# Gathers of the second batch tile without waits, and early layer-0 work placed in other units of a DLRM tower kernel

## The chip, the cores and the metric

One core of a Trainium2 chip. The metric is the device time of one execution of the program, in microseconds (us); of several executions the median is taken. The profile is of one execution.

## The reference

For 2048 samples, 32 embedding rows of 16 numbers are looked up. Three layers of a compressed interaction network follow, then a small dense tower. Cut to what matters:

```python
e = jnp.stack([tbl_f[ids[:, f]] for f in range(32)], axis=1)   # 2048 x 32 x 16
x0 = xk = e
for W in (W0, W1, W2):                                          # each 32 x (32 or 64) x 64
    xk = jax.nn.relu(jnp.einsum('bmd,bhd,mhk->bkd', x0, xk, W))
    outs.append(jnp.sum(xk, axis=2))
h = jnp.concatenate(outs + [dense_ctx], axis=1)
h = jnp.maximum(h @ W_top1 + b_top1, 0.0)
h = jnp.maximum(h @ W_top2 + b_top2, 0.0)
y = h @ W_top3
```

Everything is float32; matmuls of the layers are float32 matmuls.

## The kernel before, in words

The batch is cut into 16 tiles of 128 samples. A tile has 16 embedding columns; 128 samples times 4 columns make a block of 512 columns (64 blocks), and two blocks make a pair (32 pairs, two to a tile). The main loop runs over 256 units (L565 on ACT, L679 on DVE, L876 on PE, L384 on POOL), four units to a block, and each unit has four places i = 0 to 3. Written as (unit, i), the tables at L41 to L44 say where work on a pair is put; an entry (o, i) of pair p means unit 8(p-1)+o.

Names used below. A(n) is the DVE product of layer 1 for unit n, and B(q) that of layer 2, made in unit q+6 (L663, 128x2048 each; DVE does A(n), then B(n-6)). x1(s) and x2(s) are the outputs of layer 0 and layer 1 for block s, taken out of PSUM by ACT (L475, L490); A(4s) to A(4s+3) need x1(s), B(4s) to B(4s+3) need x2(s). Each has one buffer, so x1(s) also waits for A(4s-1) to be done and x2(s) for B(4s-1). PE multiplies each product with the weights in four contractions (L773), layer 1 on one half of the array's columns and layer 2 on the other; a contraction of layer 1 and one of layer 2 run side by side. A product of layer 1 may lie three units ahead of PE, one of layer 2 two (L661).

Layer 0 of a pair is made of squares. PE turns the pair's columns (`turn`, L699), ACT copies them (`take_x0`), PE forms sums of fields in five tiles t0 to t4 (`sum_fields`, L723), ACT squares each (`square`, L458), and PE contracts each square with a layer-0 weight (`l0_tile`, L732). Two square buffers lie between ACT and PE. When t4 is contracted, x1 of the pair's blocks can be taken. The first square of a pair also copies the fields, which an ACT DMA stores to memory; SP then loads these rows spread over the partitions into a ring of ten buffers (`keep_rows`, L264), 1 MB to a unit, and DVE reads them as one operand of A and B.

The embeddings come by 32 indirect gathers to a tile, issued by POOL (L306), into two buffers by turns. ACT casts the gathered tile to bf16 (`split_high`, L444), POOL subtracts (`split_rest`), ACT casts the rest (`split_mid`, L450), and POOL subtracts again (`split_low`); then the tile's pairs can be turned. Tile 0 is split by ACT and DVE ahead of the loop. Tile 1 is gathered in four portions that each wait for another thing (L377); then POOL runs split_rest and split_low of tile 1, and only then its loop, in which the gathers of tile 2 and later are issued a few per unit after A(n-1) is done (L390 to L395), with the additions of layer sums between them (L397 to L404).

All of this is one order written out by hand for each engine; engines work theirs in order and wait on semaphores.

```python
TURN_AT = {1: (1, 3), 2: (3, 0), 4: (0, 0)}
SPLIT_AT = {1: (9, 10), 2: (4, 5)}
```

SPLIT_AT gives the units, counted within the 16 units of a tile, in which ACT runs split_high and split_mid at i = 1: for tile 1 units 9 and 10, for tile 2 units 20 and 21. The places of x2 are made by `x2_at` (L91): x2(0) at (5, 0), x2(1) at (9, 0), x2(2) at (13, 0), x2(4) at (20, 3).

Of the kernel before, what the change touches and what calls it, by code (L numbers as in the profile page):

```python
# [14 lines left out]
B, M, D, K = 2048, 32, 16, 64  # L15
NB = 128
BT = B // NB
# [9 lines left out]
OFF = 6  # L27
# [10 lines left out]

TURN_AT = {1: (1, 3), 2: (3, 0), 4: (0, 0)}  # L41
SUMS_AT = {1: [(2, 1), (4, 0), (4, 3), (5, 1), (5, 3)], 2: [(3, 2), (4, 0), (4, 2), (5, 0), (5, 2)]}
L0_AT = {1: [(4, 1), (4, 3), (5, 1), (5, 3), (6, 1)], 2: [(4, 1), (4, 3), (5, 1), (5, 3), (6, 1)]}
X1_AT = {1: (6, 2), 2: (6, 2)}  # L44
for later in range(3, PAIRS):
    TURN_AT.setdefault(later, (-1, 1))
    SUMS_AT[later] = [(0, 2) if later == 4 else (0, 0), (1, 1), (2, 2), (4, 0), (4, 3)]
    L0_AT[later] = [(3, 0), (3, 2), (4, 2), (5, 0), (5, 2)]
    X1_AT[later] = (6, 0)


def places(table):

    at = {}
    for p, where in table.items():
        for t, (o, i) in enumerate(where if isinstance(where, list) else [where]):
            at[8 * (p - 1) + o, i] = (p, t)
    return at


TURNS, SUMS, L0S, X1S = (places(table) for table in (TURN_AT, SUMS_AT, L0_AT, X1_AT))

SPLIT_AT = {1: (9, 10), 2: (4, 5)}
for later in range(3, BT):
    SPLIT_AT[later] = (1, 4)
PIECES = 9
GROUPS = [(2 * g, 2) for g in range(7)] + [(14, 1), (15, 1)]
LAST_GROUP = len(GROUPS) - 1
# [3 lines left out]
def pieces_at():  # L72

    at = {}
    for g, (first, tiles) in enumerate(GROUPS[:-1]):
        ready = 16 * (first + tiles - 1) + 31
        for q in range(PIECES):
            if g < LAST_GROUP - 2:
# [12 lines left out]
def x2_at():  # L91

    at = {}
    for s in range(BLOCKS):
        at[(4 * s + OFF - 2, 3) if s % 2 == 0 and s >= 4 else (4 * s + OFF - 1, 0)] = s
    return at


X2S = x2_at()


# [5 lines left out]
def tower(nc, dense_t, ids, tables, w_top1, b_top1, w_top2, b_top2, w_top3, w0_pairs, w0_all, w1, w2,  # L107
          sel_sums, identity, x0_rows, out):
    with ExitStack() as ctx:
# [6 lines left out]
        def sem(name):  # L116
            return ctx.enter_context(nc.semaphore(name))
# [39 lines left out]
        at = 2 * (ST + 1) * K  # L157
# [38 lines left out]
        s_turn0 = sem("first_turned")  # L196
# [18 lines left out]
        s_prod = {1: sem("prod1_ready"), 2: sem("prod2_ready")}  # L215
        s_done = {1: sem("unit1_done"), 2: sem("unit2_done")}
        s_x = {1: sem("x1_ready"), 2: sem("x2_ready")}
# [80 lines left out]
        def _(pool):  # L298
            def gather(t, lo, hi):
                if lo == 0 and t == 2:  # L300
                    pool.wait_ge(s_high0, len(first_splits))
                    pool.wait_ge(s_rest0, len(first_splits))
                elif lo == 0 and t > 2:
                    pool.wait_ge(s_high, t - 2)
                    pool.wait_ge(s_rest, t - 2)
                for m in range(lo, hi):  # L306
                    pool.indirect_dma_start(  # L307
                        emb[t % 2][:, m, :], None, tables[m],
                        bass.IndirectOffsetOnAxis(ap=idx[:, t, m:m + 1].bitcast(U32), axis=0)
                    ).then_inc(s_early if t == 0 and m < EARLY else s_gather[t % 2], 16)  # L310

            def split_rest(t):
                pool.wait_ge(s_high, t)
                pool.tensor_tensor(rest[:, :, :], emb[t % 2][:, :, :].rearrange("p m d -> p d m"),  # L314
                                   parts[:, :, 0, :], ALU.subtract).then_inc(s_rest, 1)

            def split_low(t):
                pool.wait_ge(s_mid, t)
                pool.tensor_tensor(parts[:, :, 2, :], rest[:, :, :], parts[:, :, 1, :],
                                   ALU.subtract).then_inc(s_low, 1)  # L320
# [53 lines left out]
            gather(0, 0, M)  # L374
            pool.wait_ge(s_ids, 16)

            for k, (ready, count) in enumerate(((s_turn0, 2), (s_x[1], 1), (s_prod[1], 4), (s_prod[1], 6))):  # L377
                pool.wait_ge(ready, count)
                gather(1, k * M // 4, (k + 1) * M // 4)

            split_rest(1)
            split_low(1)
# [1 line left out]
            for n in range(10, LAST):  # L384
                t = n // 16 + 1
                if 2 <= t < BT and n % 16 == SPLIT_AT[t][0] + 1:
                    split_rest(t)
                if 2 <= t < BT and n % 16 == SPLIT_AT[t][1] + 1:
                    split_low(t)
# [19 lines left out]
        def _(act):  # L409
# [34 lines left out]
            def split_high(t):  # L444
                tile0 = M - EARLY if t % 2 == 0 else M
                act.wait_ge(s_gather[t % 2], 16 * (tile0 + M * (t // 2)))
                nc.scalar.copy(parts[:, :, 0, :], emb[t % 2][:, :, :].rearrange("p m d -> p d m"))\  # L447
                    .then_inc(s_high, 1)

            def split_mid(t):  # L450
                act.wait_ge(s_rest, t)
                nc.scalar.copy(parts[:, :, 1, :], rest[:, :, :]).then_inc(s_mid, 1)

            def take_x0(p):
                act.wait_ge(s_wide, 6 * (p - 1) + 1)
                nc.scalar.copy(x0[p % 2][:, :, :], wide[:, :, :]).then_inc(s_took, 1)  # L456
# [33 lines left out]
            def take_x2(s):  # L490
                act.wait_ge(s_done[1], 4 * s + 4)
                if s:
                    act.wait_ge(s_prod[2], 4 * s)
                if halved(1, s):
                    src = [(accs[64 * c:64 * c + 64, s % 2, 0:HALF], slice(HALF * c, HALF * c + HALF))
                           for c in range(2)]
                else:
                    src = [(accs[0:64, s % 2, :], slice(0, BLK))]
                for half in range(2):
                    for bank, cols in src:  # L500
                        last = nc.scalar.activation(xp[2][64 * half:64 * half + 64, cols], bank, ACT.Relu)  # L501
                last.then_inc(s_x[2], 1)
                if s >= 6:
                    act.wait_ge(s_z12, (s - 6) // 4 + 1)
                for bank, cols in src:
                    last = nc.scalar.activation(zin[64:128, s % 6, cols], bank, ACT.Relu)  # L506
                last.then_inc(s_xz[2], 1)

            def take_x3(s):
                act.wait_ge(s_done[2], 4 * s + 4)  # L510
                if s >= 4:
                    act.wait_ge(s_z3, s // 4)
                if halved(2, s):
                    for c in range(2):
                        last = nc.scalar.activation(x3[:, s % 4, HALF * c:HALF * c + HALF],
                                                    accs[64 * c:64 * c + 64, s % 2, 0:HALF], ACT.Relu)
                else:
                    last = nc.scalar.activation(x3[:, s % 4, :], accs[64:128, s % 2, :], ACT.Relu)  # L518
                last.then_inc(s_xz[3], 1)
# [45 lines left out]
            for n in range(LAST):  # L565
                for i in range(GT):
                    t = n // 16 + 1
                    if i == 1 and t < BT and n % 16 == SPLIT_AT[t][0]:
                        split_high(t)
                    if i == 1 and t < BT and n % 16 == SPLIT_AT[t][1]:  # L570
                        split_mid(t)
                    if (n, i) in X2S:
                        take_x2(X2S[n, i])
                    if n % 4 == (OFF + 4) % 4 and i == 0 and n >= OFF + 4:
                        take_x3((n - OFF - 4) // 4)
                    if (n, i) in TURNS:
                        take_x0(TURNS[n, i][0])
                    if (n, i) in SUMS:
                        square(*SUMS[n, i])
                    if n % 8 == 2 and i == 0 and n + 2 < UNITS:  # L580
                        take_x1((n + 2) // 4)
                    if (n, i) in X1S:
                        take_x1(2 * X1S[n, i][0])
                    if (n, i) in PIECES_AT:
                        g, q = PIECES_AT[n, i]
                        if q < 4 or q == 8:
                            take_event(g, min(q, 6))
                        elif q % 2:
                            take_event(g, 4 + (q - 4) // 2)
# [367 lines left out]
```

## Time and profile before

| | us |
|---|---|
| median of three executions | 1262.93 |
| lowest and highest of them | 1252.1 and 1274.45 |
| the profiled execution | 1259.4 |
| its span in the profile | 1257.6 |
| PE busy, DVE busy, ACT busy, POOL busy | 1204.9, 1147.8, 522.5, 682.7 |

The span is what the profile shows of the execution; the remaining 1.8 us lie around it. PE is the matmul engine, DVE the vector engine, ACT the scalar engine, POOL the gather engine here, SP the engine that issues the row loads. A float32 matmul of the program shows as two records in the trace. A matmul's record includes a modelled end, so records overlap; the step from one start to the next is the price of one.

### The profile page before, as it was taken

The numbers are of one execution on the slowest core, as the hardware profiler recorded it, in microseconds if no ns is written. First come the engines' busy times: TensorE is split into PE (matmuls) and PEld (weight loads), VectorE is DVE, ScalarE is ACT, GpSimd is POOL, SyncE is SP. The second block draws the span as 40 slices with busy tenths as digits, with TensorE's granted clock in tenths as the row PEclk, the third lists the DMA queues.
The fourth block names the chain that finished last, engine by engine and source line by source line (L and its number), as shares of the span: only waits on it lengthen the run. The fifth ranks groups of instructions, "written<-read, shape, count | busy, mean of one in ns | idle before, by whom it ended". The sixth has DMA issues, their size and how long they took to land.

```text
span 1257.6 us, 16644 instructions
## 1 busy us (share of the span) xinstructions
PE 1204.9 (96%) x6396; PEld 615.6 (49%) x6396; DVE 1147.8 (91%) x534; ACT 522.5 (42%) x786; POOL 682.7 (54%) x705
## 2 busy tenths in 40 slices
PE   0899989999999999999999999999999999999998
PEld 0442424445555555555555555555555555555444
DVE  3388989999999999999999999999999999999894
ACT  0445344434453443444344444444443444444321
POOL 6665776866767474755647375564737551210101
PEclk9999989999999999999999999999999999999998
DMA  5388978888889888898899999999998999999850
GB/s 120 78 232 224 219 197 247 248 247 236 250 237 242 235 242 239 237 240 243 226 226 229 233 246 246 248 245 236 247 243 233 228 234 241 238 235 235 210 135 1
DMA packets 73685, 277.50 MB, mean 221 GB/s; under 512 B 29819, under 2 KB 38805, under 8 KB 41318
## 3 DMA queue, kind: packets, MB, share of 16 engines
q1 hardware_dynamic: 54388, 267.09, 82.2%
q0 software_dynamic: 16384, 4.23, 3.3%
q10 hardware_dynamic: 2834, 5.12, 1.6%
q8 instruction: 51, 0.84, 0.3%
q14 instruction: 28, 0.23, 0.1%
HBM read 272.15 MB, written 4.20 MB: 220 GB/s over the span
## 4 chain that ended last, share of the span: by engine, by line
PE 88%; POOL 5%; issue 3%; DVE 2%; ACT 1%; DMA 1%; ACTq 0%; POOLq 0%; DVEq 0%
PE accs L789 66%; PE acc L743 10%; POOL emb L307 4%; PE wide L712 4%; PE xe L800 2%; DVE prod L663 2%; PE xe L809 2%; PE wide L695 1%; PE acc L856 1%; DMA emb<-in_tbl,idx 1%; PE wide L719 0%; PE wide L809 0%; PE xe L819 0%; ACT xe L501 0%; DMA idx<-in_ids 0%
## 5 line engine op out<-in xcount | busy, mean ns | idle before, releaser
L789 PE MATMUL accs<-prod,w2s 128*64 128x512 f32 x2016 | 936.3, 595 | 3.1 <-DVE prod L663 2.8
L789 PE MATMUL accs<-prod,w1s 128*64 128x512 f32 x2016 | 930.5, 594 | 0.7 <-DVE prod L663 0.7
L663 DVE TENSOR_TENSOR prod<-kept,xe 128x2048 f32<-128x2048 f32 x256 | 583.7, 2281 | 48.9 <-PE accs L789 30.9
L307 POOL DMA_INDIRECT emb<-in_tbl,idx x512 | 484.5, 946 | 204.4 <-issue 118.6
L663 DVE TENSOR_TENSOR prod<-kept,xp 128x2048 f32<-128x2048 f32 x256 | 583.1, 2279 | 6.8 <-ACT xp L482 6.8
L789 PEld LDWEIGHTS accs<-prod,w1s 128*64 128x64 f32 x2016 | 271.9, 137 | 313.6 <-issue 194.2
L789 PEld LDWEIGHTS accs<-prod,w2s 128*64 128x64 f32 x2016 | 269.8, 137 | 72.5 <-issue 40.7
L468 ACT ACTIVATE sq<-wide 128x1024 f32<-128x1024 f32 (+1 forms) x155 | 145.5, 939 | 171.9 <-PE wide L712 82.4
L743 PE MATMUL acc<-sq,u 128*64 128x512 f32 x640 | 200.5, 596 | 5.2 <-ACT sq L468 4.9
L346 POOL TENSOR_TENSOR x3f<-x3f 64x512 f32<-64x512 f32 x31 | 39.6, 1277 | 137.1 <-ACT x3f L518 136.9
L743 PEld LDWEIGHTS acc<-sq,u 128*64 128x64 f32 x640 | 82.8, 137 | 60.9 <-issue 15.7
L518 ACT ACTIVATE x3f<-accs 64x512 f32<-64x512 f32 x63 | 37.4, 593 | 126.9 <-PE accs L789 126.8
L712 PE MATMUL wide<-x,sums 128*64 128x512 bf16 x500 | 86.2, 380 | 0.6 <-ACT sq L468 0.5
L314 POOL TENSOR_TENSOR rest<-emb,parts 128x512 f32<-128x512 f32 x15 | 21.3, 1423 | 118.7 <-ACT parts L447 118.7
L501 ACT ACTIVATE xe<-accs 64x512 f32<-64x512 f32 (+1 forms) x130 | 73.1, 562 | 24.0 <-DVE prod L663 22.2
L456 ACT CAST x<-wide 128x1024 bf16<-128x1024 f32 x31 | 31.4, 1012 | 103.9 <-PE wide L695 103.9
L326 POOL TENSOR_TENSOR zin<-zin 128x512 f32<-128x512 f32 x32 | 41.2, 1286 | 59.1 <-ACT zin L506 58.8
L712 PEld LDWEIGHTS wide<-x,sums 128*64 128x64 bf16 x500 | 36.3, 110 | 67.5 <-issue 58.5
L466 ACT COPY x3f<-wide 32x1024 f32<-32x1024 f32 x31 | 31.0, 999 | 69.5 <-PE wide L712 69.4
L481 ACT ACTIVATE xp<-acc 64x512 f32<-64x512 f32 x64 | 36.4, 568 | 43.8 <-DVE prod L663 36.1
L856 PE MATMUL acc<-u 128*128 128x384 f32 x32 | 13.3, 578 | 35.5 <-DMA emb<-in_tbl,idx 35.5
L506 ACT ACTIVATE zin<-accs 64x512 f32<-64x512 f32 (+1 forms) x65 | 37.9, 583 | 1.6
(85 smaller groups left out, 510.7 us busy)
## 6 DMA issues: line engine op xcount, KB each, us to landing
kept<-x_rows SPq DMA_DIRECT2D x252, 512.0 KB, 5.3
kept<-x_rows SPq DMA_DIRECT2D x504, 256.0 KB, 6.5
emb<-in_tbl,idx POOLq DMA_INDIRECT x512, 2.6
x_rows<-x3f ACTq DMA_DIRECT2D x31, 128.0 KB, 4.7
prod<-in_w_all ACTq DMA_DIRECT2D x1, 512.0 KB, 6.7
w1s<-in_L_rec_W SPq DMA_DIRECT2D x4, 128.0 KB, 3.3
w2s<-in_L_rec_W SPq DMA_DIRECT2D x4, 128.0 KB, 3.5
wt<-in_W_top SPq DMA_DIRECT2D x1, 512.0 KB
```

The source lines that it names most:

```text
L307: pool.indirect_dma_start(emb[t % 2][:, m, :], None, tables[m], bass.IndirectOffsetOnAxis(ap=idx[:, t, m:m + 1].bitcast(U32), axis=0)).the ...
L326: pool.tensor_tensor(zin[:, a, :], zin[:, a, :], zin[:, a + 1, :], ALU.add).then_inc(s_zp, 1)
L346: pool.tensor_tensor(x3[:, a, :], x3[:, a, :], x3[:, a + 1, :], ALU.add).then_inc(s_z3p, 1)
L468: nc.scalar.activation(sq[k % 2][:, 0:n, :], wide[:, 0:n, :], ACT.Square).then_inc(s_took, 1)
L481: nc.scalar.activation(xp[1][0:64, :], src, ACT.Relu)
L501: last = nc.scalar.activation(xp[2][64 * half:64 * half + 64, cols], bank, ACT.Relu)
L506: last = nc.scalar.activation(zin[64:128, s % 6, cols], bank, ACT.Relu)
L518: last = nc.scalar.activation(x3[:, s % 4, :], accs[64:128, s % 2, :], ACT.Relu)
L663: nc.vector.tensor_tensor(prod[layer][:, q % BUFS[layer], :, :], kept[:, q % KEPT, :, :], xp[layer][:, :].unsqueeze(1).to_broadcast([128, ...
L712: last = mm(bank[64 * c:64 * c + 64, :], sums[:, t, 64 * c:64 * c + 64], x0[p % 2][:, j, :], start=True, stop=True)
L743: last = mm(acc0[64 * j:64 * j + 64, :], w, squares, start=t == 0, stop=t == ST - 1)
L789: last = mm(accs[64 * (layer - 1):64 * layer, s % 2, :], wk[layer][:, t, :], prod[layer][:, q % BUFS[layer], i, :], start=t == 0, stop=t = ...
```

## The change

- POOL issues the 32 gathers of tile 1 right behind those of tile 0, with none of the four waits.
- ACT takes x2(0) at (4, 0) where it was (5, 0).
- ACT casts tile 1 in unit 8: split_high at (8, 1), split_mid at (8, 2), where they were at (9, 1) and (10, 1).
- Pair 1 (the second): sums and squares t0 to t4 at (2,1), (3,3), (4,1), (4,3), (5,1), and layer-0 contractions at (4,0), (4,2), (5,0), (5,2), (5,3).
- Pair 2 (the third): turn at (10, 0) where it was (11, 0); sums and squares from (10, 2) to (13, 2) where they were from (11, 2) to (13, 2); layer-0 contractions from (11, 3) to (14, 0) where they were from (12, 1) to (14, 1).
- The places of later pairs, and the number of instructions of each kind, stay.

```diff
-L0_AT = {1: [(4, 1), (4, 3), (5, 1), (5, 3), (6, 1)], 2: [(4, 1), (4, 3), (5, 1), (5, 3), (6, 1)]}
+L0_AT = {1: [(4, 0), (4, 2), (5, 0), (5, 2), (5, 3)], 2: [(3, 3), (4, 1), (4, 3), (5, 2), (6, 0)]}
...
-SPLIT_AT = {1: (9, 10), 2: (4, 5)}
+SPLIT_AT = {1: (8, 8), 2: (4, 5)}
...
+MID_TILE = {1: 2}
...
-        at[(4 * s + OFF - 2, 3) if s % 2 == 0 and s >= 4 else (4 * s + OFF - 1, 0)] = s
+        at[(4, 0) if s == 0 else (4 * s + OFF - 2, 3) if s % 2 == 0 else (4 * s + OFF - 1, 0)] = s
...
-            for k, (ready, count) in enumerate(((s_turn0, 2), (s_x[1], 1), (s_prod[1], 4), (s_prod[1], 6))):
-                pool.wait_ge(ready, count)
-                gather(1, k * M // 4, (k + 1) * M // 4)
+            gather(1, 0, M)
...
-                    if i == 1 and t < BT and n % 16 == SPLIT_AT[t][1]:
+                    if t < BT and n % 16 == SPLIT_AT[t][1] and i == MID_TILE.get(t, 1):
                         split_mid(t)
```

With the new `x2_at`, x2(2) stands at (12, 3), where it was at (13, 0); at both places it comes behind the square t2 of pair 2 and ahead of t3.

Line numbers of the changed kernel are one smaller than before on ACT and PE. ACT, from the first square of pair 1 (sq) through x2(0) (xe<-accs, in four pieces), before:

```order
L468 ACTIVATE sq<-wide 128x1024
L472 DMA x_rows<-x3f 32x2x512
L468 ACTIVATE sq<-wide 128x1024 x2
L501 ACTIVATE xe<-accs 64x256 x4
L506 ACTIVATE zin<-accs 64x256 x2
L468 ACTIVATE sq<-wide 128x1024
L468 ACTIVATE sq<-wide 128x512
L481 ACTIVATE xp<-acc 64x512
```

and now:

```order
L467 ACTIVATE sq<-wide 128x1024
L471 DMA x_rows<-x3f 32x2x512
L467 ACTIVATE sq<-wide 128x1024
L500 ACTIVATE xe<-accs 64x256 x4
L505 ACTIVATE zin<-accs 64x256 x2
L467 ACTIVATE sq<-wide 128x1024 x2
L467 ACTIVATE sq<-wide 128x512
L480 ACTIVATE xp<-acc 64x512
```

x2(0) and its copy for the sums (zin) have moved ahead of the square t2, behind t1 alone.

ACT from x1(2) in unit 6 on, where parts<-emb is split_high and parts<-rest is split_mid of tile 1, before:

```order
L481 ACTIVATE xp<-acc 64x512
L482 ACTIVATE xp<-acc 64x512
L488 ACTIVATE zin<-acc 64x512
L501 ACTIVATE xe<-accs 64x512 x2
L506 ACTIVATE zin<-accs 64x512
L447 CAST parts<-emb 128x16x32
L518 ACTIVATE x3f<-accs 64x512
L481 ACTIVATE xp<-acc 64x512
L482 ACTIVATE xp<-acc 64x512
L488 ACTIVATE zin<-acc 64x512
L452 CAST parts<-rest 128x16x32
L456 CAST x_0<-wide 128x1024
```

and now:

```order
L480 ACTIVATE xp<-acc 64x512
L481 ACTIVATE xp<-acc 64x512
L487 ACTIVATE zin<-acc 64x512
L446 CAST parts<-emb 128x16x32
L451 CAST parts<-rest 128x16x32
L500 ACTIVATE xe<-accs 64x512 x2
L505 ACTIVATE zin<-accs 64x512
L517 ACTIVATE x3f<-accs 64x512
L455 CAST x_0<-wide 128x1024
L480 ACTIVATE xp<-acc 64x512
L481 ACTIVATE xp<-acc 64x512
L487 ACTIVATE zin<-acc 64x512
```

Both casts of tile 1 now stand together ahead of x2(1), and the copy of turned pair 2 (x_0<-wide) stands ahead of x1(3) (the second xp pair).

PE around the layer-0 contractions t2, t3 and t4 of pair 1 (acc<-sq,u, two matmuls each; w1s and w2s are contractions of layers 1 and 2), before:

```order
L743 MATMUL acc<-sq,u 64x512 x2
L789 MATMUL accs<-prod,w1s 64x512 x2
L719 MATMUL wide<-x_1,sums 64x512 x2
L743 MATMUL acc<-sq,u 64x512 x2
L789 MATMUL accs<-prod,w1s 64x512
L789 MATMUL accs<-prod,w2s 64x512
L789 MATMUL accs<-prod,w1s 64x512
L789 MATMUL accs<-prod,w2s 64x512
L743 MATMUL acc<-sq,u 64x512 x2
```

and now:

```order
L788 MATMUL accs<-prod,w1s 64x512
L742 MATMUL acc<-sq,u 64x512 x2
L788 MATMUL accs<-prod,w1s 64x512
L718 MATMUL wide<-x_1,sums 64x512 x2
L788 MATMUL accs<-prod,w1s 64x512
L742 MATMUL acc<-sq,u 64x512 x2
L788 MATMUL accs<-prod,w1s 64x512
L742 MATMUL acc<-sq,u 64x512 x2
L788 MATMUL accs<-prod,w1s 64x512
```

The contraction t4 has moved ahead of unit 6, whose first two pairs of contractions stood ahead of it.

## Rows read from the trace of the kernel before

**Rows 1.** Busy time by stretch, with the granted clock and DMA.

```profile
core 0: us, PE busy (x) PEld busy (x) DVE busy (x) ACT busy (x) POOL busy (x), PEclk, DMA share, GB/s
160.00:170.00 10.00, 7.84 (x26) 2.46 (x28) 8.57 (x4) 4.79 (x9) 8.16 (x9) 0.66 0.51 135
200.00:300.00 100.00, 100.00 (x502) 45.99 (x500) 99.52 (x47) 43.81 (x63) 68.28 (x71) 1.00 0.87 243
600.00:700.00 100.00, 100.00 (x528) 52.52 (x526) 97.31 (x46) 43.77 (x64) 61.18 (x63) 1.00 1.00 230
```

**Rows 2.** What DVE waited for, 58 to 182 us: total, times, longest.

```profile
DVE prod L663 <- ACT xe L501: 12.7, 4, 6.5
DVE prod L663 <- ACT xp L482: 6.8, 4, 2.3
DVE prod L663 <- PE accs L789: 0.5, 1, 0.5
```

**Rows 3.** What DVE waited for, 182 us to the end.

```profile
DVE prod L663 <- PE accs L789: 30.4, 33, 2.0
```

**Rows 4.** Timeline of DVE: start, length, and in brackets the idle time before.

```profile
78.87 2.29 DVE L663 TENSOR_TENSOR prod<-kept,xe 128x2048 f32<-128x2048 f32 x1 [3.68 <-ACT xe L501]
...
86.69 2.29 DVE L663 TENSOR_TENSOR prod<-kept,xp 128x2048 f32<-128x2048 f32 x1 [1.14 <-ACT xp L482]
...
116.77 2.29 DVE L663 TENSOR_TENSOR prod<-kept,xe 128x2048 f32<-128x2048 f32 x1 [1.43 <-ACT xe L501]
...
125.76 2.29 DVE L663 TENSOR_TENSOR prod<-kept,xp 128x2048 f32<-128x2048 f32 x1 [2.30 <-ACT xp L482]
...
160.91 2.29 DVE L663 TENSOR_TENSOR prod<-kept,xe 128x2048 f32<-128x2048 f32 x1 [6.49 <-ACT xe L501]
...
180.30 2.29 DVE L663 TENSOR_TENSOR prod<-kept,xe 128x2048 f32<-128x2048 f32 x1 [1.11 <-ACT xe L501]
```

**Rows 5.** Timeline of PE.

```profile
70.85 0.64 PE L789 MATMUL accs<-prod,w1s 128*64 128x512 f32 x1 [0.74 <-DVE prod L663]
...
105.71 0.62 PE L695 MATMUL wide<-ident_b,parts 128*128 128x128 bf16 x8 [0.23 <-POOL parts L319]
106.26 0.64 PE L789 MATMUL accs<-prod,w1s 128*64 128x512 f32 x1
...
108.02 0.60 PE L712 MATMUL wide<-x,sums 128*64 128x512 bf16 x4
108.45 0.59 PE L789 MATMUL accs<-prod,w1s 128*64 128x512 f32 x1
...
112.12 1.03 PE L743 MATMUL acc<-sq,u 128*64 128x512 f32 x4
```

**Rows 6.** Timeline of ACT.

```profile
70.03 1.02 ACT L468 ACTIVATE sq<-wide 128x1024 f32<-128x1024 f32 x1
...
77.37 1.46 ACT L501 ACTIVATE xe<-accs 64x256 f32<-64x256 f32 x4
...
85.50 0.57 ACT L481 ACTIVATE xp<-acc 64x512 f32<-64x512 f32 x1 [2.78 <-PE acc L743]
...
158.66 1.04 ACT L447 CAST parts<-emb 128x512 bf16<-128x512 f32 x1 [7.40 <-DMA emb<-in_tbl,idx]
```

**Rows 7.** Timeline of POOL.

```profile
48.47 0.94 POOL L307 DMA_INDIRECT emb<-in_tbl,idx  x1 [4.43 <-PE wide L695]
...
98.60 1.41 POOL L314 TENSOR_TENSOR rest<-emb,parts 128x512 f32<-128x512 f32 x1 [10.41 <-ACT parts L447]
104.50 1.16 POOL L319 TENSOR_TENSOR parts<-rest,parts 128x512 bf16<-128x512 f32 x1 [4.49 <-ACT parts L452]
...
144.09 1.29 POOL L326 TENSOR_TENSOR zin<-zin 128x512 f32<-128x512 f32 x1
...
148.23 0.96 POOL L307 DMA_INDIRECT emb<-in_tbl,idx  x1
...
150.74 0.94 POOL L307 DMA_INDIRECT emb<-in_tbl,idx  x1 [0.30 <-issue]
```

**Rows 8.** What SP's DMA queue waited for, whole span.

```profile
SPq L270 <- DVE prod L663: 624.8, 215, 9.4
```

More of the change, by code:

```diff
@@ L37 @@
 WARM = 16
-TURN_AT = {1: (1, 3), 2: (3, 0), 4: (0, 0)}
-SUMS_AT = {1: [(2, 1), (4, 0), (4, 3), (5, 1), (5, 3)], 2: [(3, 2), (4, 0), (4, 2), (5, 0), (5, 2)]}
-L0_AT = {1: [(4, 1), (4, 3), (5, 1), (5, 3), (6, 1)], 2: [(4, 1), (4, 3), (5, 1), (5, 3), (6, 1)]}
+TURN_AT = {1: (1, 3), 2: (2, 0), 4: (0, 0)}
+SUMS_AT = {1: [(2, 1), (3, 3), (4, 1), (4, 3), (5, 1)], 2: [(2, 2), (3, 1), (4, 0), (4, 3), (5, 2)]}
+L0_AT = {1: [(4, 0), (4, 2), (5, 0), (5, 2), (5, 3)], 2: [(3, 3), (4, 1), (4, 3), (5, 2), (6, 0)]}
 X1_AT = {1: (6, 2), 2: (6, 2)}
```

## The prediction

> **What bounds the kernel now.** Busy time by stretch comes first [rows 1]. From 200 to 300 us DVE is busy for 99.5 of 100 us, from 600 to 700 us for 97.3 of 100, with PE at 100 in both. So the early units go at the pace of DVE, the later ones at that of PE. What DVE waited for says the same: after 182 us nearly all of its waiting is for PE, 30.4 us in 33 short pieces [rows 3]; before that it waited 20.0 us, 12.7 for ACT's x2, 6.8 for x1 and 0.5 for PE [rows 2]. The change touches only units 4 to 20, which lie before 182 us. A microsecond of DVE waiting that goes there shifts all that follows, and as PE later has the same work to do from an earlier start, the end moves with it. So the sum is one over DVE's idle pieces.
>
> Each of them has its row [rows 4]: 3.68 us at 78.87 (B(0), waiting for x2(0)), 1.14 at 86.69 (A(8), x1(2)), 1.43 at 116.77 (B(8), x2(2)), 2.30 at 125.76 (A(16), x1(4)), 6.49 at 160.91 (B(16), x2(4)), 1.11 at 180.30 (B(20), x2(5)). With the 0.5 us on PE that is 16.7; most of the rest is the wait for x1(1) in unit 4, which nothing here moves. Between waits DVE runs at 2.20 us a product: from 86.69 to the wait before 116.77 thirteen products take 28.65 us, the last one's end counted in.
>
> Why B(16) is late stands with ACT and POOL. ACT was free at 158.66 - 7.40 = 151.26 and waited for tile 2's gathers before it could cast and then take x2(4) [rows 6]. The last of these gathers was issued at 150.74 [rows 7], so it landed 7.9 us later. POOL issued it so late because it had stood idle for 10.41 us, then 4.49 us, for ACT's two casts of tile 1, with tile 2's gathers queued behind [rows 7]. PE ran dry as well, and its granted clock fell: from 160 to 170 us it is busy for 7.84 us and the mean clock is 0.66, so for most of that stretch it was at 1.2 GHz, not 2.4 [rows 1].
>
> **Prices on PE** [rows 5]. A sum is 0.43 us (108.02 to 108.45), half of it for t4. From 106.26 to 108.02 stand two pairs of contractions, so a pair is about 0.86, and a layer-0 tile is four records of the same shape, 0.86 too. The turn is 0.55. A contraction of layer 1 alone also costs 0.86: half the array stands idle.
>
> **Term 1, units 4 to 8.** The square t0 of pair 1 still ends at 71.05 [rows 6]. PE does sum t1 at 71.1, now ahead of unit 4; its square ends at about 72.8, and x2(0), 1.46 us for four pieces [rows 6], at 74.3. DVE is free for B(0) at 78.87 - 3.68 = 75.2, so this wait goes. What is late next is x1(2). PE must do the eight lone contractions of units 4 and 5, five layer-0 tiles and the sums t1 to t4: 13 x 0.86 + 3 x 0.43 + 0.22 = 12.7 us, so t4 is contracted at 83.8. As a test, before it ran from 70.85 [rows 5] with 12.7 plus the two pairs of unit 6, 14.4, and x1(2) began at 85.50 [rows 6], 0.2 later. So now x1(2) begins at 84.0 and A(8) at 85.2. DVE, with B(0), A(7), B(1) done, is free at 81.8 and waits 3.4 us. Of the 4.8 us of two waits 3.4 come back as one: the gain is 1.5 us, not 4.8. Bounds: 0, if PE loses its 1.7 us at small waits, and 4.8.
>
> **Term 2, units 8 to 16.** The gathers of tile 1 begin at about 44.3 instead of 48.47 and issue every 1.25 us [rows 7], so the last goes out at 83.1 and, at the 7.9 us of tile 2's last, has landed by 91.0, likelier by 87. ACT waits for it behind x1(2) with nothing due until x2(1) at 94. Casts and subtractions (1.05, 1.4, 0.6, 1.2) are done by some 90.5, at the latest 95.5, against 105.7. The turn of pair 2 in unit 10 thus waits for nothing but B(4), which ends at 85.2 + 5 x 2.20 + 2.29 = 98.5. Then pair and turn to 99.9, ACT's copy to 101.1, x1(3) to 102.3 (A(12) wants it at 102.8), field copy and square t0 to 104.8. PE does sum t1 to 105.3, the rest of unit 11 and tile t0 to 107.9, then in unit 12 four pairs, two sums and two tiles, 6.0 us, to 113.9. The square t2 ends near 110.3. x2(2) therefore waits only for B(7), whose end is 111.7, and is out at 112.9; B(8) wants it at 85.2 + 28.65 = 113.9. The 1.43 us go. Unit 13 on PE (four pairs, sum t4, tile t3: 4.5 us) ends at 118.4, pair and tile t4 at 120.1, x1(4) at 121.5. DVE is free for A(16) after three products, at 120.5, and waits 1.0 of its former 2.30. A(16) comes at 121.5 against 125.76: 4.3 us are gained so far, 2.8 of them here. Bounds for this term: 0 (one slip of PE behind a square) and 3.7.
>
> **Term 3, unit 20.** POOL is free for tile 2 from 90.5, but a gather waits for A(n-1), three or four a unit, so it goes with DVE now. Units 10 to 18 hold 29 gathers; in unit 18 also the additions, 4.1 us (144.09 to 148.23 [rows 7]). POOL begins the four gathers of unit 17 at about 124.3, those of unit 18 at 129.3, and after the additions the last three at 137.2; the last goes out at 139.7, 11 us earlier. Landing takes 7.9 us if it is as slow as before: 147.6. ACT arrives at 151.26 - 4.3 = 147.0. DVE, free at 121.5 + 28.65 = 150.2, needs x2(4) then, so the cast must start by 150.2 - 1.15 - 1.05 = 148.0. It does, with 0.4 us to spare at the slowest landing that the rows show. All 6.49 us go. Bounds: 3 us, if the landing takes over 11 us, and 6.49.
>
> On this landing the Trainium skill (DMA: Bandwidth & Descriptors, section Anatomy of one DMA — SWDGE (gpsimd) path) gives 2.0 us plus bytes over 436 GB/s; for a gather of 8 KB that is an estimate of 2.0 us, by which the last would land at 141.7, the sum would stay as it is and the rival of a late landing would fall away. The trace has 7.9 us at this place, so the rival keeps its chance.
>
> **Term 4, after the stall.** The 0.5 us on PE and part of the 1.11 us at B(20) come from PE's half clock and the backlog of it. I take 1.1 of 1.6; bounds 0 and 1.6.
>
> **Sum.** 1.5 + 2.8 + 6.5 + 1.1 = 11.9 us. The profiled execution took 1259.4 (span 1257.6), so 1247.5; I say 1248. The profiled one is 3.5 us below the median of 1262.93, of which 1248 is 1.2% less.
>
> **Rivals.**
> - The placing does nothing: PE in units 4 to 14 slips at each square and terms 1 and 2 are 0. For it speaks that they rest on margins of about a microsecond; against it that no wait of theirs takes PE's place in the chain worked out above. 1259.4 - 6.5 - 1.1 = 1251.8.
> - The gathers of tile 2 still land late: past 148.0 each microsecond of landing costs one. Kept are terms 1 and 2 alone: 1259.4 - 4.3 = 1255.1. For it the 0.4 us margin, against it the 11 us of earlier issue.
> - The row loads become the bound, from unit 10 to the end. A unit needs 1.05 MB in 4.40 us, 238 GB/s; 243 were moved from 200 to 300 us and 230 from 600 to 700. There DVE's 97.31 us busy are 44.2 products, 22.1 units, so PE's pace is 4.52 us a unit [rows 1]. Should 228 be all that comes, a unit takes 4.60 us: 0.20 more than DVE's over units 10 to 47, 7 us, and 0.08 more than PE's over the 208 units behind, 17 us: 1248 + 24 = 1272, slower than before. It decides at about 230 GB/s (4.55 us a unit), where the 11.9 us are used up. Against it: the loads waited 624.8 us for DVE to free a buffer [rows 8], so the 230 is what was asked for, and none of DVE's waits before 182 us is for a load [rows 2].
> - More goes than I count: all of the 16.7 us, 1259.4 - 16.7 = 1242.7; against it the 12.7 us of PE work in term 1.
>
> **Chances.** Forecast 0.61, placing without effect 0.14, late landing 0.14, row loads 0.04, all waits gone 0.07. From 1242.7 to 1255.1 hold nearly all of it; but three executions of the same kernel lie 22 us apart, 0.9% to either side of their median, so the range goes some 8 us beyond either end: 1236 to 1263. Two per cent of the median, about what a measurement of this kernel can tell from no change, is 25 us: no case reaches 1237.7, only scatter on top of a full gain does. Faster by over 2%: 0.11; within: 0.86; slower: 0.03.
>
> **What would show it.** DVE should have one wait of about 3.4 us before A(8) at 85, one of about 1 before A(16), none at B(0), B(8) and B(16); ACT no wait for gathers in unit 20; POOL's gathers of tile 1 in one row from 44 to 84 us; PE's clock full from 150 to 180 us. Wrong would be: x2(4) still behind the gathers, A(8) still at 86.7, a DVE wait on row loads, or a gain that is there at 182 us and gone at 300.

## The result and the profile after

| | before | after |
|---|---|---|
| median of 20 executions each, us | 1259.84 | 1252.38 |
| lowest and highest, us | 1252.1 and 1274.45 | 1247.48 and 1265.31 |
| the profiled execution, us | 1259.4 | 1254.39 |
| its span, us | 1257.6 | 1252.6 |

The ratio of the times, which leaves out executions over 1.5% above the fastest of their kernel, is 0.9944, with a 95% interval from 0.9924 to 0.9965: faster by 0.6%, some 7 us, which lies within 2%. The forecast was 1248 in a range from 1236 to 1263.

What DVE waited for from 58 to 182 us, after (total, times, longest):

```profile
DVE prod L662 <- ACT xp L481: 7.2, 4, 3.3
DVE prod L662 <- ACT xe L500: 1.8, 2, 1.1
DVE prod L662 <- PE accs L788: 0.6, 1, 0.6
```

Those are 9.6 us, against 20.0 before [rows 2]. x2 costs 1.8 us where it cost 12.7; x1 has gone up from 6.8 to 7.2 (3.3 us of either are A(0)'s 2.04 and A(4)'s 1.28, which the change leaves alone). The timeline of DVE shows the places:

```profile
84.69 2.29 DVE L662 TENSOR_TENSOR prod<-kept,xp 128x2048 f32<-128x2048 f32 x1 [3.30 <-ACT xp L481]
...
118.45 2.29 DVE L662 TENSOR_TENSOR prod<-kept,xe 128x2048 f32<-128x2048 f32 x1 [0.55 <-PE accs L788]
121.32 2.29 DVE L662 TENSOR_TENSOR prod<-kept,xp 128x2048 f32<-128x2048 f32 x1 [0.58 <-ACT xp L481]
...
151.09 2.29 DVE L662 TENSOR_TENSOR prod<-kept,xe 128x2048 f32<-128x2048 f32 x1 [1.11 <-ACT xe L500]
...
169.48 2.29 DVE L662 TENSOR_TENSOR prod<-kept,xe 128x2048 f32<-128x2048 f32 x1 [0.72 <-ACT xe L500]
```

They are A(8), B(9), A(16), B(16) and B(20). The waits of 3.68 us at B(0) and 1.43 at B(8) [rows 4] are gone; B(16) keeps 1.11 of 6.49. ACT after:

```profile
72.38 1.46 ACT L500 ACTIVATE xe<-accs 64x256 f32<-64x256 f32 x4
...
83.51 0.57 ACT L480 ACTIVATE xp<-acc 64x512 f32<-64x512 f32 x1 [2.78 <-PE acc L742]
...
91.39 1.09 ACT L446 CAST parts<-emb 128x512 bf16<-128x512 f32 x1 [6.22 <-DMA emb<-in_tbl,idx]
...
148.79 1.09 ACT L446 CAST parts<-emb 128x512 bf16<-128x512 f32 x1 [1.97 <-DMA emb<-in_tbl,idx]
```

x2(0) is taken at 72.38 instead of 77.37, x1(2) at 83.51 instead of 85.50, and the last cast starts at 148.79 instead of 158.66 [rows 6]. POOL after:

```profile
82.97 0.94 POOL L308 DMA_INDIRECT emb<-in_tbl,idx  x1 [0.30 <-issue]
92.56 1.41 POOL L315 TENSOR_TENSOR rest<-emb,parts 128x512 f32<-128x512 f32 x1 [8.64 <-ACT parts L446]
94.70 1.16 POOL L320 TENSOR_TENSOR parts<-rest,parts 128x512 bf16<-128x512 f32 x1 [0.73 <-ACT parts L451]
96.02 0.95 POOL L308 DMA_INDIRECT emb<-in_tbl,idx  x1 [0.15 <-DVE prod L662]
...
140.92 0.94 POOL L308 DMA_INDIRECT emb<-in_tbl,idx  x1 [0.31 <-issue]
```

The last gather of tile 1 (82.97), the two subtractions of tile 1, the first gather of tile 2 (96.02) and its last (140.92; 150.74 before [rows 7]). Busy time by stretch, in the columns of [rows 1]:

```profile
160.00:170.00 10.00, 9.78 (x53) 3.75 (x51) 9.28 (x5) 4.70 (x6) 8.46 (x9) 1.00 1.03 245
200.00:300.00 100.00, 99.04 (x494) 45.77 (x492) 96.87 (x45) 44.42 (x64) 67.12 (x69) 1.00 1.03 233
600.00:700.00 100.00, 100.00 (x530) 52.62 (x528) 98.12 (x46) 43.51 (x64) 60.41 (x63) 1.00 0.96 243
```

From 160 to 170 us PE is at 2.4 GHz throughout (1.00; 0.66 before) and busy for 9.78 us instead of 7.84. But from 200 to 300 us DVE is busy for 96.87 us instead of 99.52, and the DMA share is 1.03 at 233 GB/s, where it was 0.87 at 243 [rows 1]. What is missing there stands in DVE's waits after 182 us:

```profile
DVE prod L662 <- PE accs L788: 27.1, 29, 2.0
DVE prod L662 <- DMA kept<-x_rows: 7.2, 21, 0.7
```

The second row is new: 7.2 us in 21 pieces for the row loads. Before has no such row.

**Where the 5.0 us between the two profiled spans come from.** Take A(30), the seventh product behind B(20), whose wait is the last that the change touches, and B(255), the last product of all. On DVE's timeline, before:

```profile
195.69 2.28 DVE L663 TENSOR_TENSOR prod<-kept,xp 128x2048 f32<-128x2048 f32 x1
...
1238.96 4.48 DVE L663 TENSOR_TENSOR prod<-kept,xe 128x2048 f32<-128x2048 f32 x2
```

and after:

```profile
184.88 2.28 DVE L662 TENSOR_TENSOR prod<-kept,xp 128x2048 f32<-128x2048 f32 x1
...
1238.74 2.28 DVE L662 TENSOR_TENSOR prod<-kept,xe 128x2048 f32<-128x2048 f32 x1
```

The row of 1238.96 holds B(254) and B(255); B(255) starts 2.20 later, at 1241.16. A(30) starts at 195.69 before and 184.88 after, 10.8 us earlier, 0.5 of which A(0) already had (58.31 and 57.80; over all the profiles of this document it lies between 57.8 and 59.0). From A(30) to B(255) before takes 1045.47 us and after 1053.86: 8.4 us lost. The end behind B(255) is 2.6 us shorter after. 0.5 + 10.3 - 8.4 + 2.6 = 5.0. The last term is the clock: one group of matmuls near the end, on PE's timeline, before:

```profile
1250.62 3.68 PE L809 MATMUL wide<-h,wt 128*64 128x128 f32 x32 [0.69 <-ACT h L539]
```

and after:

```profile
1247.73 1.97 PE L808 MATMUL wide<-h,wt 128*64 128x128 f32 x32 [0.69 <-ACT h L538]
```

The same 32 matmuls took 3.68 us at 1.2 GHz (granted clock 0.50 from 1250 to 1254 us) and 1.97 at 2.4 (1.00). Behind B(255) a profile takes either 13.8 us or 16.4 to 16.8, and both kernels have both: the changed one has the long end in e4 and e9 below, the kernel before the short one in e6. So the 2.6 us are not put down to the change. The 8.4 us are the question of the experiments.

### The profile page after: what moved, and what is told of

Its sections match the earlier page's. It is cut to its first block, busy times and chain, and to the rows that moved or that the text cites. A ratio compares the mean times of both kernels' runs of the same rounds, so it can differ in the third digit from the quotient of the medians.

```text
span 1252.6 us, 16643 instructions
## 1 busy us (share of the span) xinstructions
PE 1204.9 (96%) x6396; PEld 606.0 (48%) x6396; DVE 1150.4 (92%) x534; ACT 522.6 (42%) x786; POOL 682.9 (55%) x705
## 4 chain that ended last, share of the span: by engine, by line
PE 72%; DMA 12%; DVE 6%; POOL 5%; issue 4%; SPq 1%; ACT 0%; DVEq 0%; ACTq 0%
PE accs L788 54%; DMA kept<-x_rows 11%; PE acc L742 9%; DVE prod L662 6%; POOL emb L308 5%; PE wide L711 3%; PE xe L799 2%; PE xe L808 2%; PE wide L694 1%; SPq L271 1%; DMA emb<-in_tbl,idx 1%; PE wide L718 0%; PE xe L818 0%; DMA idx<-in_ids 0%; PE accs L784 0%
## 5 line engine op out<-in xcount | busy, mean ns | idle before, releaser
L742 PE MATMUL acc<-sq,u 128*64 128x512 f32 x640 | 218.9, 593 | 0.3 <-ACT sq L437 0.3
L711 PE MATMUL wide<-x,sums 128*64 128x512 bf16 x500 | 90.0, 380 | 1.1 <-ACT sq L467 1.0
```

Of the source, the lines that this page charges most:

```text
L711: last = mm(bank[64 * c:64 * c + 64, :], sums[:, t, 64 * c:64 * c + 64], x0[p % 2][:, j, :], start=True, stop=True)
L742: last = mm(acc0[64 * j:64 * j + 64, :], w, squares, start=t == 0, stop=t == ST - 1)
```

## The experiments

Theory A: the loads take back what the change gains, since products that come earlier ask for rows earlier than they can come; the kernel before loses nothing to them. The theory that stood in the end, D in the later expectations: the loads have slow stretches that come and go in either kernel, so an execution loses between 0 and 16 us whether or not the change is in it. Every time below is a median of several executions unless it is said to be one execution; losses, waits and distances from A(0) are each read from one profile. All products and the row loads are found again by their order, so "loss" below always means the time from A(30) to B(255) less 1045.4 us, which is what it takes when no product waits for a load.

**e1 and e2: a quarter of the row loads left out.** In both kernels the last of the three row loads of a unit (32 of 128 partitions) is left out from unit 14 on; the products there use what an earlier unit left in the ring.

```diff
-                for r, lo, hi in PARTS:
+                for r, lo, hi in PARTS if n < KEPT + MADE else PARTS[:2]:
...
-                        dve.wait_ge(s_kept[q % KEPT], 48 * loads)
+                        dve.wait_ge(s_kept[q % KEPT], 48 + 32 * (loads - 1))
```

Before with it:

> The kernel before, with the last of the three row loads of a unit (256 KB of 1 MB, partitions 96 to 127) left out from unit 14 on, so these partitions hold old rows. Theory A (in the changed kernel the row loads take back most of what was gained, and only because DVE no longer pauses; in the kernel before they cost nothing): DVE had no wait on a load before, so the time stays within 0.4% of before, 1254 to 1262 us; the wait at B(16), where tile 2's gathers land late, may shrink from 6.5 us to some 3. Theory B (the loads bound both kernels all along): over 8 us faster than before, under 1251.

Measured: 1253.27 us, ratio 0.9937 [0.9909, 0.9966], loss 0. Both theories' numbers were missed by a little: the kernel before had no load wait to lose in its first profile, and still gained. 6.0 us of the gain are at A(30), and they come from the gathers. Timeline of ACT, e1:

```profile
153.94 1.08 ACT L447 CAST parts<-emb 128x512 bf16<-128x512 f32 x1 [2.32 <-DMA emb<-in_tbl,idx]
```

The last gather of tile 2 was issued at 151.07 and the cast ran at 153.94: landed 2.9 us after its issue, not 7.9. The wait before B(16) shrank from 6.49 to 1.45 us. So 5.0 us of the stall that the change removes were themselves the work of the row loads, which hold the gathers up.

After with it:

> The changed kernel with the same load left out from unit 14 on. Theory A: no DVE wait on a load, the gain of 10.8 us that the changed kernel shows at A(30) is kept to the end: 1245 to 1249 us, 0.990 to 0.993 of before. Rival C (it is PE or ACT that gives the gain back between 250 and 585 us): DVE waits on PE there instead, and the time stays near 1252.

Measured: 1245.67 us, ratio 0.9879 [0.9827, 0.9932], loss 0, as either theory has it once the loads are light; A(30) is 126.05 us behind A(0), against 137.38 in before and 131.35 in e1. Busy time by stretch, e2:

```profile
200.00:300.00 100.00, 100.00 (x504) 48.33 (x502) 98.74 (x46) 45.60 (x67) 68.98 (x71) 1.00 0.62 189
```

With the DMA share at 0.62 nothing waits for a load, and the whole early gain arrives at B(255) (by the clock of the span, 10.85 us ahead of before at A(30) and 10.91 there). Against e1 the change is worth 7.6 us between medians; in the profiles it is 5.3 at A(30), the rest being the clock of the tail, which costs e1 2.6 us (3.68 us for the 32 matmuls, 1.97 in e2). Between the executions with a mean granted clock of 0.999 or more (five of e1, three of e2) the medians are 1250.5 and 1245.5, 5.0 apart.

**e3: the gathers and casts alone.** The changed kernel with the old tables for pairs 1 and 2 and the old places of x2(0) and x2(2).

```diff
-SUMS_AT = {1: [(2, 1), (3, 3), (4, 1), (4, 3), (5, 1)], 2: [(2, 2), (3, 1), (4, 0), (4, 3), (5, 2)]}
+SUMS_AT = {1: [(2, 1), (4, 0), (4, 3), (5, 1), (5, 3)], 2: [(3, 2), (4, 0), (4, 2), (5, 0), (5, 2)]}
...
-        at[(4, 0) if s == 0 else (4 * s + OFF - 2, 3) if s % 2 == 0 else (4 * s + OFF - 1, 0)] = s
+        at[(4 * s + OFF - 2, 3) if s % 2 == 0 and s >= 4 else (4 * s + OFF - 1, 0)] = s
```

> The kernel before with the new gathers of tile 1 and the casts in unit 8, but all pairs and x2(0) at their old places. If the four terms are right: waits at B(0) 3.7, A(8) 1.1, B(8) about 1 and A(16) about 2 us stay, the one at B(16) falls from 6.5 to under 1, A(30) starts 6.5 to 8 us earlier than before, near 188 us. Theory A: then loads take part of it back and the end comes at 1253 to 1257. If the places were needed for it: the wait at B(16) stays above 3 us.

Measured: 1257.21 us, ratio 0.9961 [0.9927, 0.9994]. The waits at B(0), A(8), B(8) and A(16) stand (3.68, 1.14, 1.14, 2.30 us), that at B(16) is gone, and A(30) comes 129.77 us after A(0), 7.6 earlier than before: just terms 3 and 4 of the sum. Its profile then lost 14.4 us.

**e4: the changed kernel again.** No edit.

> The changed kernel, unchanged, in another execution. Theory A: DVE again waits for row loads somewhere between 200 and 600 us, 4 to 10 us in all, and the gain of some 11 us at A(30) is down to 3 to 6 at the end. Rival D (a slow stretch of the memory that the first profile met by chance): no such waits, or at another place, and the gain at the end is 9 us or more.

Measured: 1255.66 us, ratio 0.9953 [0.9912, 0.9993]. Its profile gained as much by A(30) (127.03 us from A(0)) and lost 15.8. What DVE waited for from 182 us on, e4:

```profile
DVE prod L662 <- DMA kept<-x_rows: 12.8, 25, 1.2
```

That is more than either expectation had: 13 of the pieces lie between 203 and 317 us, the other 12 between 954 and 1035. Busy time by stretch, e4:

```profile
700.00:750.00 50.00, 50.00 (x280) 27.85 (x277) 47.66 (x23) 21.25 (x33) 29.78 (x31) 1.00 0.84 236
950.00:1000.00 50.00, 47.36 (x243) 24.46 (x240) 43.65 (x20) 19.45 (x29) 28.54 (x30) 1.00 1.03 214
```

From 700 to 750 us the loads have room: 236 GB/s at a share of 0.84, and DVE waits for none from 600 to 900. From 950 to 1000 they bring 214 GB/s at a share of 1.03, and DVE is busy for 43.65 us instead of 47.66. The loop asks for 1 MB of rows a unit at both places.

**e5 and e6: the kernel before, two more executions.** No edit.

> The kernel before, unchanged, in another execution. Theory A (DVE's pauses before 182 us keep the ring of row buffers full, so loads never cost the kernel before anything): no DVE wait on a load, as in its first profile. Theory D (stretches in which the memory serves the loads more slowly come at any time and cost either kernel): in at least one of two such looks DVE waits for loads over 3 us in all, after 182 us. The wait at B(16) for tile 2's gathers should be 4 to 8 us in both theories.

> The same again, a third execution of the kernel before: theory A no DVE wait on a load, theory D over 3 us in this one or the other. The wait at B(16) 4 to 8 us.

Measured: one execution each, 1265.21 and 1269.75 us, losses 4.9 and 12.0; B(16) waits 5.81 and 6.80 us, as expected. What DVE waited for from 182 us on, e5:

```profile
DVE prod L663 <- PE accs L789: 29.3, 32, 2.0
DVE prod L663 <- DMA kept<-x_rows: 4.6, 9, 0.8
```

and e6:

```profile
DVE prod L663 <- PE accs L789: 27.8, 31, 2.0
DVE prod L663 <- DMA kept<-x_rows: 10.2, 15, 1.8
```

Busy time by stretch, e6:

```profile
700.00:750.00 50.00, 50.00 (x277) 28.65 (x275) 47.66 (x23) 21.31 (x33) 26.53 (x27) 1.00 0.85 235
950.00:1000.00 50.00, 46.44 (x235) 21.37 (x233) 43.49 (x21) 18.77 (x28) 30.75 (x33) 1.00 1.03 213
```

213 GB/s at a share of 1.03, as in e4 at the same place, where the first profile of before moves 236 GB/s at 0.98 and has no such wait. Theory A falls in its second half: the kernel before loses to the loads too. Its first profile, on which the prediction was built, was an execution that lost nothing.

**e7: pair 1 alone.** The kernel before with the new places of pair 1 and x2(0) at (4, 0).

```diff
-L0_AT = {1: [(4, 1), (4, 3), (5, 1), (5, 3), (6, 1)], 2: [(4, 1), (4, 3), (5, 1), (5, 3), (6, 1)]}
+L0_AT = {1: [(4, 0), (4, 2), (5, 0), (5, 2), (5, 3)], 2: [(4, 1), (4, 3), (5, 1), (5, 3), (6, 1)]}
```

(with the new SUMS_AT of pair 1 and the x2(0) place likewise)

> The kernel before with only pair 1's new places and x2(0) at (4, 0). By term 1 the wait at B(0) goes, the one at A(8) grows to 3.3 us, and A(8) starts 26.9 us after A(0) instead of 28.4, 1.5 us earlier. The waits at B(8) 1.4, A(16) 2.3 and B(16) 4 to 8 us stay. The rival, that PE loses it to small waits: A(8) 28.4 us after A(0).

Measured: one execution, 1270.16 us. Timeline of DVE, e7:

```profile
85.42 2.29 DVE L663 TENSOR_TENSOR prod<-kept,xp 128x2048 f32<-128x2048 f32 x1 [3.30 <-ACT xp L482]
...
115.60 2.29 DVE L663 TENSOR_TENSOR prod<-kept,xe 128x2048 f32<-128x2048 f32 x1 [1.43 <-ACT xe L501]
...
124.59 2.29 DVE L663 TENSOR_TENSOR prod<-kept,xp 128x2048 f32<-128x2048 f32 x1 [2.30 <-ACT xp L482]
...
159.86 2.29 DVE L663 TENSOR_TENSOR prod<-kept,xe 128x2048 f32<-128x2048 f32 x1 [6.61 <-ACT xe L501]
```

A(8) waits 3.30 us and comes 26.89 us after A(0), as in the changed kernel and 1.5 earlier than before; B(8), A(16) and B(16) wait as before. A(30) is 2.0 us nearer to A(0). Then 15.2 us went to loads: a part of the change that gains 2 us came out 11 us over the first profile of before. A single execution of this kernel says nothing on a change of this size.

**e8 and e10: one more buffer in the ring.** The changed kernel with eleven buffers instead of ten, to ride out short slow stretches.

```diff
-KEPT = 10
+KEPT = 11
```

> The changed kernel with eleven row buffers in place of ten. If it is short slow stretches of the loads that run the ring dry, one more unit of lead (4.4 us) takes a good part of the waits away: median 1247 to 1251 us, 0.989 to 0.993 of before. If the loads fall behind by a rate over long stretches, one more buffer only puts the first wait off: 1251 to 1256 us, 0.994 to 0.997.

> Eleven row buffers again, now beside the changed kernel on the same chip. If the additional lead takes away part of the waits on loads: its median 2 to 5 us under that of the changed kernel. If the loads fall behind by a rate over long stretches: within 2 us of it.

Measured: 1250.23 us, 0.9926 [0.9889, 0.9963], and 1248.52, 0.991 [0.9875, 0.9945]; losses 5.0 and 1.6. e10 is 3.0 us under e9 below, on the same chip, but the intervals overlap: not settled.

**e9: the changed kernel, five rounds.** No edit.

> The changed kernel, unchanged, as the measure for the other three of this set. By the looks so far: A(30) 10 to 11 us earlier than before counted from A(0), DVE waits on row loads of 5 to 16 us in one profiled execution, median 1251 to 1256 us.

Measured: 1251.53 us, 0.9912 [0.9882, 0.9941]. Here B(16) has no wait at all, A(30) comes 126.06 us after A(0), and the loss is 4.0 us, a little under what was expected. It ran on another chip than e4, and no run tells whether the chip has a part in the 4 us between their medians.

**e11: the lone contractions halved.** Eleven buffers, and layer 1 of block 1 is contracted in two halves, one on each side of the array.

```diff
-    return (layer, s) in ((1, 0), (2, BLOCKS - 1))
+    return (layer, s) in ((1, 0), (1, 1), (2, BLOCKS - 1))
...
-                if t == 0 and (layer, s) in ((2, 0), (2, BLOCKS - 1)):
+                if t == 0 and (layer, s) in ((2, 0), (2, 1), (2, BLOCKS - 1)):
```

> Eleven row buffers, and block 1's layer-1 contractions (units 4 to 7) cut into two halves of 256 columns side by side on both halves of the array, as block 0's are. If the lone contractions set x1(2), as term 1 has it: units 4 and 5 cost PE 8 x 0.43 = 3.4 us less, the wait at A(8) falls from 3.3 us to under 1.5, and A(8) starts 23.5 to 25 us after A(0) instead of 26.9; units 6 and 7 then cost PE 3.4 us more, where a contraction of layer 2 no longer runs beside a whole one, so of the 3.3 us only 0 to 3 are left at A(30). Rival: x1(2) hangs on the chain of squares on ACT, and the wait at A(8) stays over 2.5 us.

Measured: 1248.56 us, 0.9893 [0.9866, 0.9921], loss 0.1. Timeline of DVE, e11:

```profile
82.15 2.29 DVE L662 TENSOR_TENSOR prod<-kept,xp 128x2048 f32<-128x2048 f32 x1 [0.83 <-ACT xp L481]
86.12 2.29 DVE L662 TENSOR_TENSOR prod<-kept,xe 128x2048 f32<-128x2048 f32 x1 [1.68 <-PE accs L788]
...
91.28 2.29 DVE L662 TENSOR_TENSOR prod<-kept,xe 128x2048 f32<-128x2048 f32 x1 [0.68 <-PE accs L788]
...
96.71 2.29 DVE L662 TENSOR_TENSOR prod<-kept,xe 128x2048 f32<-128x2048 f32 x1 [0.94 <-ACT xe L500]
```

The wait before A(8) falls from 3.30 to 0.83 us and A(8) comes 24.30 us after A(0), as it should if the lone contractions set x1(2), which is what term 1 says. But products now wait 1.68 and 0.68 us for PE and 0.94 for x2: A(30) stands 127.66 us after A(0), 0.6 later than after the change. Nothing is gained there, where 0 to 3 us were expected; that its median is among the lowest goes with the ring or with chance.

**e12: a pause put in.** The changed kernel with A(23) done four times, three products of 2.3 us more.

```diff
-                nc.vector.tensor_tensor(prod[layer][:, q % BUFS[layer], :, :], kept[:, q % KEPT, :, :],
...
+                for k in range(4 if (layer, q) == (1, 23) else 1):
```

> The changed kernel with the product A(23) done four times over, a pause of 6.6 us for all others at the place where the kernel before stood still. Theory A (a pause lets the ring of row buffers fill, so that less is lost to loads later): the 6.6 us come back and the median is within 2.5 us of the changed kernel. Theory D (slow stretches come at any time, in either kernel alike): the median is 5 to 8 us above the changed kernel's, near the time of the kernel before.

Measured: 1260.48 us, ratio 1.0005 [0.997, 1.004], 9 us above e9 on the same chip. A(30) comes 135.67 us after A(0), 8.6 more than after the change: 7.0 for the pause, the rest in longer waits around it. The 9 us are a microsecond past theory D's number and far from theory A's 2.5. The loss in the one profile is 2.0, 2.0 less than in e9, which the spread of the losses covers; by the medians nothing comes back. If the loads alone set the end, a later start would have cost nothing. So it counts when the products start, and theory A's number falls here as well.

This is also the one profile of the fourteen in which DVE waits for row loads ahead of A(30), 4.2 us in three pieces. The longest is before A(8), which comes 0.3 us later by it:

```profile
85.27 2.29 DVE L666 TENSOR_TENSOR prod<-kept,xp 128x2048 f32<-128x2048 f32 x1 [3.59 <-DMA kept<-x_rows]
```

## Why the prediction was right, point by point

All counted from A(0), so that the head of the kernel stays out of it; the measured is that of the first profile after.

| step | forecast | measured |
|---|---|---|
| term 1, A(8) | 1.5 | 28.38 - 26.89 = 1.5 |
| wait left before A(8) | 3.4 | 3.30 |
| term 2, A(16) | 2.8 more | 67.45 - 63.52 - 1.5 = 2.4 |
| term 3, B(16) | 6.5 more | 102.60 - 93.29 - 3.9 = 5.4 |
| term 4, A(30) | 1.1 more | 137.38 - 127.08 - 9.3 = 1.0 |
| sum | 11.9 | 10.3 |

- **Term 1** came out to a tenth, its reason too: x2(0) moved out of the way, the eight lone contractions remain (e7, e11).
- **Term 2** fell short by 0.4. POOL's split of tile 1 ended at 95.86, 0.4 past the late bound of the forecast (95.5) and not at the likely 90.5, as the last gather landed 8.4 us after its issue (82.97 to 91.39). But that cost nothing: PE turns pair 2 behind B(4), whose end is at 98.1 (its row on PE stands below this item). What was late is PE further on: x1(4) is taken out from 120.14 on, where the forecast, less the 0.5 of A(0), has 119.8. The 0.55 us for PE before B(9) were not foreseen; before A(16) 0.58 remain. Together 1.1, where 1.0 was said. No run has pair 2's new places alone, so this term is read in place only.

```profile
99.18 0.62 PE L694 MATMUL wide<-ident_b,parts 128*128 128x128 bf16 x8
```

- **Term 3** fell short by 1.1: the last gather was issued at 140.92 (forecast 139.7) and landed 7.9 us later, at 148.79, past the limit of 148.0. The rival of a late landing was thus right by a microsecond. In e2 and e9 the wait is gone; in e9 the last gather landed 6.8 us after its issue. The estimate of 2.0 us that the prediction made from the Trainium skill (DMA: Bandwidth & Descriptors, Anatomy of one DMA — SWDGE (gpsimd) path) does not hold here beside full row loads, where 7.9 us were measured; with a quarter of them left out, 2.9 us (e1) come nearer. It comes within 0.4 us for the gathers of tile 0 issued from 20 to 33 us, ahead of the first row load (53.9 us), with the DMA share at 0.06. Shortest, median and longest landing of these, before:

```profile
DMA to landing us min/median/max: 2.2/2.3/2.4
```

- **PE's clock** from 160 to 170 us is back at 2.4 GHz, as said.
- **The step that failed** is "as PE later has the same work to do from an earlier start, the end moves with it". Row loads lie between the start and the end. They cost 8.4 us in the first profile after, 15.8 and 4.0 in its two repeats, and 0, 4.9 and 12.0 in three of before. The prediction read "none of DVE's waits before 182 us is for a load" off one execution and gave the loads a chance of 0.04, as a steady bound that decides at about 230 GB/s and costs 24 us at 228. They are not steady: the waits come in stretches of some 10 to 150 us, which differ from execution to execution. Some places come back: e3, e4, e6 and e9, four of the ten profiles with such waits, have a stretch between 920 and 1035 us, in either kernel. "A DVE wait on row loads" was one of the prediction's own signs of being wrong, and it came. What the prediction called scatter is in part this; how large a part was not measured.
- **The time itself**, 1252.38 against 1248, is this near in part by luck. The sum started from a profile that happened to lose nothing, so the loads' toll was missing at the end, and the terms were 1.6 us too large; but that profile also had the long end, 2.6 us, which works the other way: in 17 of the 20 executions after, the mean granted clock is 0.999 or more.
- One small misreading: of the 3.3 us of waits that the prediction leaves out, most is A(0)'s 2.04 us, not the wait for x1(1) in unit 4, 1.28. The sum does not use either.
- Whether the change makes the loads dearer on average is open: three losses of each kernel with a spread of twelve microseconds do not tell. The medians lean that way: lighter loads took 6.7 us off the kernel before (1260.00, taken beside e1, to 1253.27), 6.0 of which already stand at A(30), and 6.7 to 10.0 off the changed one (1252.38 and e4's 1255.66 to e2's 1245.67), only 1.0 of which stands there. With four executions of e2 that is no finding. e2 against e1, both free of it, says what the change is worth where nothing waits for a load and gathers land early: 5.3 us from A(0) to A(30). Beside full loads it was 10.3 to 11.3 there (after, e4, e9 against the first profile of before).

## What to carry to other kernels

Before a sum over one profile is trusted to the end, profile several executions of the kernel before: a resource that is within a few per cent of its limit may show no wait in one and 12 us in the next. When a stall ends at a transfer, ask what the transfer was late behind; here 5.0 of 6.5 us came from other transfers, and either an earlier issue or lighter traffic removes it. Experiments on a few microseconds are read at a fixed instruction (here A(30) counted from A(0)), where they agree within a microsecond, not at the end, where they differ by 16.

## What the runs showed of the hardware that was not expected

- The rate at which the DMA engines move data, most of it row loads, varies within an execution of one loop: 235 to 236 GB/s at a share of 0.84 to 0.85 without a wait, and 213 to 214 at 1.03 with DVE waiting (e4, e6). When it happens differs from execution to execution, though four of ten profiles have such waits between 920 and 1035 us. What causes it was not found.
- The last gather of tile 1 or 2 landed 6.8 to 8.9 us after its issue beside full row loads (share 0.91 to 1.04), in e1 with a quarter of them left out 2.9 us (share 0.54 from 150 to 154 us), and gathers ahead of the row loads in 2.2 to 2.4 (share 0.06).
- Near the end PE idles 2.04 us for DVE; in nine of the fourteen profiles the last matmuls then run at a granted clock of 0.50, 1.2 GHz, which costs 2.6 us, and in five it stays at 1.00, in the same kernel.
